# Four buffers for scaled rows and a new order of work in the first chunks of two routed feed-forward stages

## The chip, the cores and the metric

The kernel runs on one core of a Trainium2 chip. The metric is the device time of one execution in microseconds (us), median of the runs. All times in a profile are counted from the start of its span.

## The reference

```python
x = x + 0.5 * ffn(layernorm(x))          # first FFN stage, routed
x = x + attention(layernorm(x))          # 32 sequences of 512 rows, causal, one head of 256
x = x + 0.5 * ffn(layernorm(x))          # second FFN stage, same weights

def ffn(x):                               # T = 16384 rows of 256, E = 8 experts, cap = T // E = 2048
    xn = rmsnorm(x) * norm_weight
    probs = softmax(xn @ router_w.T + router_b)
    gates, idx = top_k(probs.T, cap)      # each expert takes its 2048 best rows
    hmid = gelu(xn[idx] @ fc1_w.T + fc1_b)            # 256 -> 1024, per expert
    ye = hmid @ fc2_w.T + fc2_b                       # 1024 -> 256
    out = zeros.at[idx].add(ye * gates)
    gate_sums = zeros.at[idx].add(gates)
    return out / max(gate_sums, 1e-9)
```

## The kernel before, in words

The program has four parts: a scan of x that gives router logits (to about 85 us), the choice of the rows and the first FFN stage (to about 835 us), attention (to about 1300 us), the choice and the second FFN stage (to the end). The five engines have a program each; they meet through semaphores, and each engine's order of work is written by hand. Products in float32 quality are made of three float16 products (high by high, high by low, low by high), so each value is split into a high and a low half.

**An FFN stage** is 32 chunks of 512 chosen rows, four chunks an expert. In the code N0 and E0 are the first chunk and first expert of the stage, m is the chunk within the stage, and t one of four blocks of a chunk. TensorE runs in block (m, t): two slices of `fc1` of chunk m (12 matmuls, 2.6 us), then `fc2` of chunk m-1 for 128 rows (24 matmuls, 2.6 us). A chunk needs, in this order:

- *its slot list*: TensorE's `pick` (four small matmuls) and VectorE's `count_slots` turn the counts of chosen rows into row numbers (`tok`, `gate_at`). `pick(E, q)` waits for `tiles` and for the `count_slots` of the list before it.
- *its rows*: GpSimd's `gather`, 4 indirect DMAs, into one of two buffers `xe`. It waits for the slot list.
- *its scale* (first stage only, since there the layer norm is still to be made): VectorE's `rows_stats` (4 BN_STATS, 4 BN_AGGR, then `cx`), GpSimd's `roots` (`zsx`, a power of -0.5), VectorE's `rows_shift` (`zbx`).
- *its split rows*: ScalarE's `rows_hi` and VectorE's `rows_lo` write `xs`, and SyncE's queue transposes them into `xt` (`columns`).
- `fc1`, then ScalarE's `gelu` (to `hf` and `hid_h`) and VectorE's `hidden_lo` (`hid_l`), then `fc2`, then VectorE's `y_bias` (`yb`).
- *its gates*: GpSimd's `weights`, 4 indirect DMAs that read the list `gate_d` in DRAM; ScalarE's `y_out` multiplies `yb` by them into the scaled rows `ys`; GpSimd's `scatter`, 4 indirect DMAs, adds `ys` to the rows in DRAM.

ScalarE works in order too. In the first block of chunk m it does two gelus, then the `y_out` that are due there (`scaled(m, t)`: chunk 0's four blocks at (2, 3), chunk 1's at (3, 0) and (3, 1), from chunk 5 on one a block, just behind), then `rows_hi` of chunk m+1, then goes on with gelu. `fc1` slice f writes one of three PSUM banks, so slice 3 of chunk m waits for gelu 0, and slice 5 for gelu 2 of that chunk: two slices can run ahead of a ScalarE that waits.

**The choice for experts 1 to 7** is finished while chunks 0 and 1 already run: `choice_3` to `choice_8` on VectorE, and between them TensorE's `other_limits` at (1, 0) and `other_places` at (1, 3), which waits for `choice_7`. From the finished mask, GpSimd's `gate_sums` and `gates` and VectorE's `gate_scale` make the normalised gates, SyncE writes them to `gate_d`, and `weights` reads them.

GpSimd's order in a stage is the program of `ffn_rows`: one engine issues every gather, weights and scatter DMA and computes the roots, and while it waits for one of them, none behind it starts.

## Time and profile before

| | us |
|---|---|
| median of 3 runs (2070.72 to 2072.58) | 2071.78 |
| the profiled execution | 2071.05 |
| its span | 2069.2 |
| TensorE busy in the span | 1951.3 (94%) |
| VectorE, ScalarE, GpSimd busy | 1449.0, 1398.8, 1259.4 |
| mean granted TensorE clock | 0.98 |

The time of an execution is its span and 1.85 us around it. The profile comes from one execution; 0.98 of the clock is a mean over stretches at full clock and a few at half.

### The profile page before, as it was taken

To read this page: it belongs to the slowest core of one execution; us is meant where nothing else is said; L and a number is where in the kernel's file an instruction comes from. 1 tells how busy PE (TensorE), PEld (TensorE's weight loads), DVE (VectorE), ACT (ScalarE), POOL (GpSimd) and SP (SyncE) were. 2 spreads that over 40 slices of the span, in tenths; PEclk is the share of its full clock that TensorE was granted. 3 is DMA by queue.
4 is the path that set the end of the run, shared out by engine and by line. 5 is a ranking of instruction groups with operands and counts; after the bars stand their busy time and mean duration, and the time that the engine had idled before them with its cause. 6 is when DMAs were issued, how large, how long until landed. Compare 5 with 4: busy or idle time off the path is not lost. (4 is left out here: it accounts for less than half of the span.)

```text
span 2069.2 us, 42505 instructions
## 1 busy us (share of the span) xinstructions
PE 1951.3 (94%) x15382; PEld 1352.3 (65%) x15382; DVE 1449.0 (70%) x4271; ACT 1398.8 (68%) x2680; POOL 1259.4 (61%) x1437
## 2 busy tenths in 40 slices
PE   8858999999999999799999999669999999999997
PEld 6534666666666666577777777435666666666665
DVE  7778777777777765488899998677555555656542
ACT  8635676766767676578888787455576676666663
POOL 8224887777777776644444442027877676767674
PEclk9979999999999999999999999989999999999999
DMA  9943565646565545655555554234655555646453
GB/s 289 346 123 92 114 101 91 106 89 131 85 108 92 100 76 69 116 134 154 159 159 163 135 150 116 85 77 105 107 115 89 107 108 87 131 85 106 71 77 36
DMA packets 361744, 242.33 MB, mean 117 GB/s; under 512 B 228928, under 2 KB 348992, under 8 KB 361280
## 3 DMA queue, kind: packets, MB, share of 16 engines
q1 hardware_dynamic: 304192, 172.34, 31.7%
q0 software_dynamic: 57344, 67.29, 22.4%
q8 instruction: 122, 2.00, 0.4%
q14 instruction: 86, 0.70, 0.1%
HBM read 121.03 MB, written 84.93 MB: 100 GB/s over the span
## 5 line engine op out<-in xcount | busy, mean ns | idle before, releaser
L1273 DVE SCALAR_TENSOR_TENSOR hid_l<-hf,hid_h 128x512 f16<-128x512 f32 x512 | 352.3, 699 | 341.4 <-ACT hid_h L719 340.0
L1494 PE MATMUL ps<-w_h,hid_h 128*128 128x256 f16 x2048 | 559.2, 273 | 0.0
L1495 PE MATMUL ps<-w_l,hid_h 128*128 128x256 f16 x2048 | 559.1, 273 | 0.0
L1496 PE MATMUL ps<-w_h,hid_l 128*128 128x256 f16 x2048 | 558.9, 273 | 0.0
L1494 PE MATMUL ps<-xt,w_h 128*128 128x512 f16 x1024 | 389.8, 381 | 19.4 <-ACT hf L820 14.3
L820 ACT ACTIVATE hf<-ps,b 128x512 f32<-128x512 f32 x512 | 345.1, 674 | 78.5 <-PE ps L1496 72.1
L1496 PE MATMUL ps<-xt,w_l 128*128 128x512 f16 x1024 | 389.9, 381 | 0.0
L1495 PE MATMUL ps<-xt,w_h 128*128 128x512 f16 x1024 | 389.7, 381 | 0.0
L719 ACT ACTIVATE ys<-yb,weight 128x256 f32<-128x256 f32 x256 | 128.0, 506 | 342.6 <-DVE yb L1291 336.2
L719 ACT ACTIVATE hid_h<-hf 128x512 f16<-128x512 f32 x512 | 322.5, 630 | 16.2
L606 POOL DMA_INDIRECT weight<-gate_d,gate_at x256 | 257.7, 1007 | 84.1 <-issue 76.5
L616 POOL DMA_INDIRECT out<-ys,tok x128 | 207.5, 1621 | 113.0 <-ACT ys L719 77.1
L1494 PEld LDWEIGHTS ps<-w_h,hid_h 128*128 128x128 f16 x2048 | 200.8, 98 | 50.5 <-issue 0.5
L1495 PEld LDWEIGHTS ps<-w_l,hid_h 128*128 128x128 f16 x2048 | 200.7, 98 | 50.2 <-issue 0.5
L616 POOL DMA_INDIRECT x_d<-ys,tok x128 | 207.7, 1623 | 37.3 <-issue 36.7
L1496 PEld LDWEIGHTS ps<-w_h,hid_l 128*128 128x128 f16 x2048 | 200.7, 98 | 23.5
L596 POOL DMA_INDIRECT xe<-x,tok x128 | 132.1, 1032 | 103.6 <-DVE gate_at L1228 65.7
L596 POOL DMA_INDIRECT xe<-z_d,tok x128 | 137.2, 1072 | 93.6 <-issue 93.4
L1496 PEld LDWEIGHTS ps<-xt,w_l 128*128 128x128 f16 x1024 | 100.5, 98 | 121.9 <-issue 1.9
L1494 PEld LDWEIGHTS ps<-xt,w_h 128*128 128x128 f16 x1024 | 100.6, 98 | 117.5 <-ACT hf L820 16.8
L1495 PEld LDWEIGHTS ps<-xt,w_h 128*128 128x128 f16 x1024 | 100.5, 98 | 93.6 <-issue 1.4
L1291 DVE TENSOR_TENSOR yb<-ps,b_now 128x256 f32<-128x256 f32 x256 | 107.4, 420 | 62.9 <-PE ps L1496 61.2
(289 smaller groups left out, 3818.1 us busy)
## 6 DMA issues: line engine op xcount, KB each, us to landing
w_st<-fc_t SPq DMA_DIRECT2D x32, 1024.0 KB
xin<-x SPq DMA_DIRECT2D x32, 512.0 KB, 6.1
xa<-x_d SPq DMA_DIRECT2D x32, 512.0 KB, 4.6
out<-x SPq DMA_DIRECT2D x32, 512.0 KB, 5.2
z_d<-z SPq DMA_DIRECT2D x32, 512.0 KB, 6.1
xt<-xs SPq DMA_TRANSPOSE x256
weight<-gate_d,gate_at POOLq DMA_INDIRECT x256, 2.4
b_st<-fc_b SPq DMA_DIRECT2D x16, 128.0 KB
```

Of the source, the lines that this page charges most:

```text
L596: pool.indirect_dma_start(xe[:, n % 2, t, :], None, rows, bass.IndirectOffsetOnAxis(ap=tok[:, E % 3, k:k + 1].bitcast(U32), axis=0)).then_ ...
L606: pool.indirect_dma_start(weight[:, E % 3, k:k + 1], None, gate_d, bass.IndirectOffsetOnAxis(ap=gate_at[:, E % 3, k:k + 1].bitcast(U32), a ...
L616: pool.indirect_dma_start(acc, bass.IndirectOffsetOnAxis(ap=tok[:, E % 3, k:k + 1].bitcast(U32), axis=0), ys[:, n % 2, t, :], None, comput ...
L719: return act.activation(dst, src, ACT.Copy, **kw)
L820: act.activation(hf[:, f % HF, :], bank(FC1[f % 3]), ACT.Gelu, bias=b1[:, e, f:f + 1], scale=1.0 / WS).then_inc(s_gelu, 1)
L1273: dve.scalar_tensor_tensor(hid_l[:, n % 2, f, :], hf[:, f % HF, :], HS, hid_h[:, n % 2, f, :], ALU.mult, ALU.subtract).then_inc(s_hl, 1)
L1291: dve.tensor_tensor(yb[:, n % 2, t, :], bank(4 + t % 2)[:, 0:D], b2_now[:, n // NC % 2], ALU.add).then_inc(s_yb, 1)
L1494: pe.matmul(dst, lh, rh, start=first, stop=False)
L1495: pe.matmul(dst, lh, rl, start=False, stop=False)
L1496: return pe.matmul(dst, ll, rh, start=False, stop=last)
```

## The change

- **Four buffers of scaled rows.** `ys` had two. Two more (`ys_more`) are laid over `above` and `scan`, which are free once the choice is done. Chunk n uses buffer n mod 4, with a semaphore of its own, so `y_out` of chunk n waits for the scatter of chunk n-4, no longer n-2.
- **Gate sum.** GpSimd keeps one multiplication (`chosen`); its three additions go. VectorE adds the eight experts in one reduction over a view of `gate` whose neighbouring elements lie 512 bytes apart. `gate_scale` moves from behind `tiles` at (1, 3) to (1, 2), ahead of `choice_7`.
- **First chunks' slot list, statistics, roots, gathers.** The fourth list (`pick` and `count_slots`) moves from chunk 1 to chunk 0. `rows_stats` of chunk 1 moves ahead of `choice_2` and the low halves of the fc2 weights, that of chunk 3 from the end of (1, 3) to (1, 2). GpSimd gets the order shown below.
- **Scatters.** The chunk in which two are issued is m = 6, was m = 4; the early scatters ahead of the roots go.
- **Weight load swapped.** SyncE issues the second expert's fc2 weights ahead of the store of `gate_d`, not behind it.

```diff
+    YS_RING = 4
...
-            return {2: [0], 3: [1], 4: [2, 3]}.get(m, [m - 1])
+            return {2: [0], 3: [1], 4: [2], 5: [3], 6: [4, 5]}.get(m, [m - 1])
...
+                w2_in(E0 + 1)
                 sp.wait_ge(s_gate, layer + 1)
                 sp.dma_start(gate_d.rearrange("(e t p) a -> t e (p a)", e=NE, p=P), gate[:, :, :]).then_inc(s_gate_d, 16)
-                w2_in(E0 + 1)
...
-            def gate_sums(layer):
+            def chosen(layer):
 
                 pool.wait_ge(s_mask, layer + 1)
-                steps.link(pool.tensor_tensor(gate[:, :, :], equal[:, :, :], p_r[:, :, :], ALU.mult))
-                steps.link(pool.tensor_tensor(gsum[:, :, :], gate[:, 0:NE // 2, :], gate[:, NE // 2:NE, :], ALU.add))
...
+                pool.tensor_tensor(gate[:, :, :], equal[:, :, :], p_r[:, :, :], ALU.mult).then_inc(s_gsum, 1)
...
+                roots(N0 + 1)
                 gather(N0 + 2)
-                roots(N0 + 1)
                 roots(N0 + 2)
-                gate_sums(layer)
                 gather(N0 + 3)
+                chosen(layer)
+                roots(N0 + 3)
                 gates(layer)
-                roots(N0 + 3)
+                gather(N0 + 4)
                 pool.wait_ge(s_gate_d, 16 * (layer + 1))
                 weights(N0)
                 weights(N0 + 1)
...
                 for m in range(2, LAST + 1):
-                    if m + 2 < LAST:
+                    if 4 <= m and m + 2 < LAST:
                         gather(N0 + m + 2)
                     if m < LAST:
                         weights(N0 + m)
-                    early = scattered(m)[:1] if m in (3, 4) else []
-                    for n in early:
-                        scatter(N0 + n)
                     if m + 2 < LAST:
                         roots(N0 + m + 2)
+                    if m == 2:
+                        gather(N0 + 5)
...
-                        for n in scattered(m)[len(early):]:
+                        for n in scattered(m):
                             scatter(N0 + n)
...
-                link(dve.tensor_scalar(ginv[:, :], gsum[:, 0, :], 1e-9, None, ALU.max))
+                link(dve.tensor_reduce(ginv[:, :], gate[:, :, :].rearrange("p e t -> p t e"), AX.X, ALU.add))
+                link(dve.tensor_scalar(ginv[:, :], ginv[:, :], 1e-9, None, ALU.max))
...
+                    if (m, t) == (0, 3):
+                        count_slots(0, E0, 3)
...
                     if (m, t) == (1, 1):
                         choice_6(layer)
-                        count_slots(0, E0, 3)
                     if (m, t) == (1, 2):
+                        rows_stats(E0 * NC + 3)
+                        gate_scale(layer)
                         choice_7(layer)
                     if (m, t) == (1, 3):
                         choice_8(layer)
                         tiles(1, E0 + 1, 0, 1)
-                        gate_scale(layer)
...
                 count_slots(0, E0, 2)
+                rows_stats(N0 + 1)
```

GpSimd in the first stage, from the roots of chunk 3 to those of chunk 4. `xe<-x,tok` is a gather, `weight<-gate_d,gate_at` a weights DMA, `zsx<-cx` a roots. Before:

```order
L582 TENSOR_TENSOR gate<-gate,ginv 128x1024 [waits s_ginv]
L623 TENSOR_TENSOR zsx<-cx,minus_half 128x4 [waits s_cx]
L606 DMA weight<-gate_d,gate_at 128x1 [waits s_gate_d,s_idx]
L606 DMA weight<-gate_d,gate_at 128x1 x3
L606 DMA weight<-gate_d,gate_at 128x1 [waits s_idx]
L606 DMA weight<-gate_d,gate_at 128x1 x3
L596 DMA xe<-x,tok 128x256 [waits s_xsl,s_copy,s_idx]
L596 DMA xe<-x,tok 128x256 x3
L606 DMA weight<-gate_d,gate_at 128x1 [waits s_idx]
L606 DMA weight<-gate_d,gate_at 128x1 x3
L623 TENSOR_TENSOR zsx<-cx,minus_half 128x4 [waits s_cx]
```

And after:

```order
L624 TENSOR_TENSOR zsx<-cx,minus_half 128x4 [waits s_cx]
L583 TENSOR_TENSOR gate<-gate,ginv 128x1024 [waits s_ginv]
L597 DMA xe<-x,tok 128x256 [waits s_idx,s_xsl]
L597 DMA xe<-x,tok 128x256 x3
L607 DMA weight<-gate_d,gate_at 128x1 [waits s_gate_d,s_idx]
L607 DMA weight<-gate_d,gate_at 128x1 x3
L607 DMA weight<-gate_d,gate_at 128x1 [waits s_idx]
L607 DMA weight<-gate_d,gate_at 128x1 x3
L607 DMA weight<-gate_d,gate_at 128x1 [waits s_copy,s_idx]
L607 DMA weight<-gate_d,gate_at 128x1 x3
L624 TENSOR_TENSOR zsx<-cx,minus_half 128x4 [waits s_cx]
```

Chunk 4's gather stood behind the weights of chunks 0 and 1 and now stands ahead of them. It waits (`s_idx`) for the first slot list of expert 1, made in block (2, 1), and all three weights and the roots of chunk 4 stand behind it.

VectorE in the first stage, block (1, 2), up to the row that releases `other_places` (the third after the scan). `hid_l` is `hidden_lo`, `seen` to `gate_at` a `count_slots`, `bstx` to `cx` a `rows_stats`. Before, from the end of (1, 1):

```order
L1215 TENSOR_SCALAR seen,found<-ps,slot_id 128x127 [waits s_pick,s_mask]
L1215 TENSOR_SCALAR seen,found<-ps,slot_id 128x127 x3
L1219 TENSOR_TENSOR tok_f<-found,ps 128x4 [waits s_dve]
L1227 CAST tok<-tok_f 128x4 [waits s_seen]
L1228 TENSOR_SCALAR gate_at<-tok_f,first_row 128x4
L1273 SCALAR_TENSOR_TENSOR hid_l<-hf,hid_h 128x512 [waits s_hh] x2
L1291 TENSOR_TENSOR yb<-ps,b_now 128x256 [waits s_y]
L1180 SCALAR_TENSOR_TENSOR scan<-equal 128x896
```

And after:

```order
L1275 SCALAR_TENSOR_TENSOR hid_l<-hf,hid_h 128x512 [waits s_hh,s_mask]
L1275 SCALAR_TENSOR_TENSOR hid_l<-hf,hid_h 128x512 [waits s_hh]
L1293 TENSOR_TENSOR yb<-ps,b_now 128x256 [waits s_y]
L1250 BN_STATS bstx<-xe 128x6 [waits s_xe1]
L1250 BN_STATS bstx<-xe 128x6 x3
L1253 BN_AGGR mvx<-bstx 128x2 [waits s_dve]
L1253 BN_AGGR mvx<-bstx 128x2 x3
L1255 TENSOR_SCALAR cx<-mvx 128x4 [waits s_dve]
L1196 TENSOR_REDUCE ginv<-gate 128x128 [waits s_gsum]
L1197 TENSOR_SCALAR ginv<-ginv 128x128 [waits s_dve]
L1198 RECIPROCAL ginv<-ginv 128x128 [waits s_dve]
L1199 TENSOR_SCALAR ginv<-ginv 128x128 [waits s_dve]
```

The slot list has left this place for chunk 0; chunk 3's statistics and the whole gate scale now stand ahead of the scan. In the second stage the same holds without `bstx` to `cx`.

GpSimd in the first stage, chunk 6, with the first rows of chunk 7. Before, one scatter stands between the roots of chunk 8 and the gather of chunk 9; after, there are two:

```order
L624 TENSOR_TENSOR zsx<-cx,minus_half 128x4 [waits s_cx]
L617 DMA x_d<-ys,tok 16384x256 [waits s_ys]
L617 DMA x_d<-ys,tok 16384x256 x3
L617 DMA x_d<-ys,tok 16384x256 [waits s_ys]
L617 DMA x_d<-ys,tok 16384x256 x3
L597 DMA xe<-x,tok 128x256 [waits s_idx,s_xsl]
L597 DMA xe<-x,tok 128x256 x3
```

Those rows are of the changed program; the four scatter DMAs of chunk 5 are what moved in ahead of the gather.

## Rows read from the trace of the kernel before

**Rows 1.** Busy time by stretch: length, PE, PEld, DVE, ACT, POOL, clock, DMA share, GB/s

```profile
200.00:250.00 50.00, 45.45 (x307) 29.92 (x305) 39.46 (x125) 30.36 (x54) 38.01 (x34) 0.93 0.54 121
350.00:400.00 50.00, 50.00 (x356) 34.35 (x355) 35.98 (x111) 36.53 (x63) 35.14 (x31) 1.00 0.46 85
1400.00:1450.00 50.00, 45.35 (x312) 30.10 (x310) 38.97 (x98) 29.90 (x55) 37.56 (x30) 0.97 0.46 106
```

**Rows 2.** TensorE's timeline, first stage: start, duration, operation, idle before and releaser

```profile
191.60 0.39 PE L1620 MATMUL ps<-per_expert,before 128*128 128x7 f32 x2 [1.44 <-DVE per_expert L1182]
208.07 0.61 PE L1494 MATMUL ps<-xt,w_h 128*128 128x512 f16 x1 [4.13 <-ACT hf L820]
...
231.81 0.38 PE L1494 MATMUL ps<-xt,w_h 128*128 128x512 f16 x1
...
246.96 0.40 PE L1659 MATMUL ps<-counts,tile_of 128*128 128x128 f16 x4 [0.42 <-DVE tile_of L1208]
...
255.46 0.39 PE L1494 MATMUL ps<-xt,w_h 128*128 128x512 f16 x1 [1.60 <-ACT hf L820]
261.97 0.38 PE L1659 MATMUL ps<-counts,tile_of 128*128 128x128 f16 x4 [2.42 <-DVE tok_f L1219]
```

**Rows 3.** TensorE's timeline, second stage

```profile
1424.72 0.55 PE L1494 MATMUL ps<-xt,w_h 128*128 128x512 f16 x1 [4.62 <-ACT hf L820]
...
1491.20 0.39 PE L1494 MATMUL ps<-xt,w_h 128*128 128x512 f16 x1 [0.77 <-ACT hf L820]
```

**Rows 4.** ScalarE's timeline, both stages

```profile
206.81 0.63 ACT L719 ACTIVATE w_h<-w_st 128x512 f16<-128x512 f32 x1 [2.54 <-DMA w_st<-fc_t]
...
1415.22 1.33 ACT L719 ACTIVATE xs<-xe 128x256 f16<-128x256 f32 x4 [3.09 <-DMA xe<-z_d,tok]
1423.46 0.63 ACT L719 ACTIVATE w_h<-w_st 128x512 f16<-128x512 f32 x1 [6.90 <-DMA w_st<-fc_t]
...
1488.85 0.51 ACT L719 ACTIVATE ys<-yb,weight 128x256 f32<-128x256 f32 x1 [6.38 <-DMA out<-ys,tok]
```

**Rows 5.** VectorE's timeline, first stage; its last row is of the second

```profile
167.11 1.08 DVE L1163 TENSOR_REDUCE per_expert<-above 128x7 f32<-128x896 f32 x1
...
188.86 2.21 DVE L1180 TENSOR_TENSOR_SCAN scan<-equal 128x896 f32<-128x896 f32 x1
...
195.76 0.95 DVE L1196 RECIPROCAL ginv<-ginv 128x128 f32<-128x128 f32 x1
...
212.51 0.39 DVE L1228 TENSOR_SCALAR gate_at<-tok_f,first_row 128x4 int32<-128x4 f32 x1
...
1429.12 0.22 DVE L1228 TENSOR_SCALAR gate_at<-tok_f,first_row 128x4 int32<-128x4 f32 x1
```

**Rows 6.** GpSimd by line, 188 to 400 us; then one row of its timeline

```profile
L616 POOL DMA_INDIRECT x_d<-ys,tok x37 | 61.2, 1654 | 10.4 <-issue 10.1 <-ACT ys L719 0.3
L606 POOL DMA_INDIRECT weight<-gate_d,gate_at x44 | 44.5, 1011 | 15.2 <-issue 13.1 <-DMA gate_d<-gate 2.1
...
250.84 1.62 POOL L623 TENSOR_TENSOR zsx<-cx,minus_half 128x4 f32<-128x4 f32 x1
```

**Rows 7.** GpSimd's roots of chunk 8; gathers' and weights' landing; VectorE, chunk 7's end

```profile
313.08 1.05 POOL L623 TENSOR_TENSOR zsx<-cx,minus_half 128x4 f32<-128x4 f32 x1 [2.77 <-DVE cx L1253]
...
DMA to landing us min/median/max: 2.7/3.0/3.3
...
weight<-gate_d,gate_at POOLq DMA_INDIRECT x256, 2.4
...
331.38 1.39 DVE L1248 BATCH_NORM_STATS2 bstx<-xe 128x6 f32<-128x256 f32 x4
...
334.55 0.43 DVE L1208 TENSOR_TENSOR tile_of<-tile_of,below 128x512 f16<-128x512 f16 x1
```

**Rows 8.** Busy time by stretch, as rows 1, around two idle times of TensorE

```profile
209.00:220.00 11.00, 11.00 (x70) 7.35 (x69) 7.79 (x21) 8.11 (x16) 8.30 (x9) 0.81 0.50 155
1424.00:1429.00 5.00, 4.28 (x18) 2.31 (x19) 2.95 (x12) 4.87 (x10) 3.78 (x5) 0.66 0.36 59
```

More of the change, by code:

```diff
@@ L183, in macaron @@
         gate = sb("gate", [P, NE, P], F32, ffn)
-        gsum = sb("gsum", [P, NE // 2, P], F32, ffn)
         ginv = sb("ginv", [P, P], F32, ffn)
@@ L190, in macaron @@
         p_r = sb("p_r", [P, NE, P], F32, ffn)
-        above = sb("above", [P, NE, P], F32, ffn)
         equal = sb("equal", [P, NE, P], F32, ffn)
-        scan = sb("scan", [P, NE, P], F32, ffn)
+        choice = ExitStack()
+        above = sb("above", [P, NE, P], F32, choice)
+        scan = sb("scan", [P, NE, P], F32, choice)
+        choice.close()
+        ys_more = sb("ys_more", [P, 2, TG, D], F32, ffn)
         w1_h = sb("w1_h", [P, 2, KD, FF], F16, ffn)
@@ L299, in macaron @@
         s_xe = [sem("s_xe0"), sem("s_xe1")]
-        s_sc = [sem("s_sc0"), sem("s_sc1")]
+        s_sc = [sem(f"s_sc{u}") for u in range(YS_RING)]
         s_xt = [sem("s_xt0"), sem("s_xt1")]
@@ L361, in final_rows @@
             for n in (FINAL - NC + g - 1, FINAL - NC + g):
-                engine.wait_ge(s_sc[n % 2], 16 * TG * (n // 2 + 1))
+                engine.wait_ge(s_sc[n % YS_RING], 16 * TG * (n // YS_RING + 1))
         def flat(t):
@@ L707, in _ @@
             ffn_rows(1, z_d, outf)
-            for u in range(2):
-                pool.wait_ge(s_sc[u], 16 * TG * NC * NE)
+            for u in range(YS_RING):
+                pool.wait_ge(s_sc[u], 16 * TG * (2 * NC * NE // YS_RING))
             pool.sem_inc(s_phase, 1)
@@ L842, in y_out @@
                         act.wait_ge(s_weight[c], 16 * TG * (E + 1))
-                        wait(act, s_sc[n % 2], 16 * TG * (n // 2))
+                        wait(act, s_sc[n % YS_RING], 16 * TG * (n // YS_RING))
                     act.wait_ge(s_yb, TG * n + t + 1)
-                    copy(ys[:, n % 2, t, :], yb[:, n % 2, t, :], scale=weight[:, E % 3, k:k + 1]).then_inc(s_ys, 1)
+                    copy(scaled_rows(n)[:, t, :], yb[:, n % 2, t, :], scale=weight[:, E % 3, k:k + 1]).then_inc(s_ys, 1)
                 act.activation(warm[:, :], nws[:, 0:1], ACT.Gelu)
@@ L1221, in count_slots @@
                 if q == 0:
-                    for u in range(2):
-                        wait(dve, s_sc[u], 16 * TG * (NC // 2) * (E - 2))
+                    for u in range(YS_RING):
+                        wait(dve, s_sc[u], 16 * TG * (NC // YS_RING) * (E - 2))
                     for c in range(NC):
@@ L1348, in ffn @@
                     w2_lo(E0, h)
-                rows_stats(N0 + 1)
                 for m in range(LAST + 1):
@@ L1366, in ffn @@
                             first_turns(m, t)
-                        if t == 3 and m + 2 < LAST:
+                        if t == 3 and m + 2 < LAST and m != 1:
                             rows_stats(n + 2)
@@ L1682, in ffn @@
                             pick(ahead, 2 * c + t // 2)
+                        if (m, t) == (0, 1):
+                            pick(E0, 3)
                         if (m, t) == (1, 0):
                             other_limits(layer)
-                            pick(E0, 3)
                         if (m, t) == (1, 3):
```

9 lines of the change are left out of this document (3 added, 6 removed).

## The prediction

> **What bounds the kernel now.** I read the busy time by stretch first. In steady state, 350 to 400 us, TensorE (PE) is busy for all of 50.00 us at a granted clock of 1.00, the upper of its two levels (2.4 GHz), and no other engine passes 36.53 [rows 1]. There only TensorE's own work counts, and the change leaves that alone. What can move are the two heads: 200 to 250 us has 4.55 us of idle TensorE and a clock of 0.93, 1400 to 1450 us 4.65 us and 0.97 [rows 1]. Then TensorE's timeline, for the names of these idle times. First stage: 1.44 us until VectorE's per-expert counts of choice_7, 4.13 until a gelu at 208.07, and in chunk 4 0.42, 1.60 and 2.42 [rows 2]. Second stage: 4.62 at 1424.72 and 0.77 at 1491.20, both until a gelu [rows 3]. ScalarE's timeline says why the gelus are late: it had waited for the fc2 weights of the second expert, 2.54 us at 206.81 and 6.90 at 1423.46, for the gather of chunk 3 (3.09 at 1415.22), and for a scatter to free one of the two buffers (6.38 at 1488.85) [rows 4]. After the two long idle times the clock falls to the lower level (1.2 GHz) for a while: 11.00 us at a mean of 0.81 and 5.00 at 0.66 [rows 8], which cost (1 - 0.81) x 11 = 2.1 us and (1 - 0.66) x 5 = 1.7 us.
>
> So the question is for which of the other engines TensorE waits in the two heads after the change. A chunk takes TensorE four blocks of 5.2 us and a few picks, about 21 us. A move is worth something only where it shortens or lengthens one of its waits.
>
> **Block (1, 2), first stage.** Moved ahead of choice_7 on VectorE: rows_stats of chunk 3, 2.0 us (1.39 for its BN_STATS, as at 331.38 [rows 7], 0.6 for the aggregates), and the gate scale: reciprocal 0.95 [rows 5] and two short operations, 1.4 in all, and the new reduction over 1024 elements. The trace has no reduction with elements 512 bytes apart; the nearest row reduces 896 elements in 1.08 us [rows 5], so 1024 take 1.23. Above it the bound is the slowest VectorE rate over such a tile, the scan, 2.21 for 896 [rows 5], so 2.5; below, 1.1. I take 1.23, since the work is of the kind of the first row. Sum 4.6. Gone from ahead of choice_7 is the slot list, 2.55 us here (1.7, and 0.85 for one slow CAST), of which VectorE would now spend up to 1.1 waiting for gelus, so it gives back 1.45 to 2.55: choice_7 ends 2.1 to 3.2 later. I take 2.4, 193.9 and not 191.5, and TensorE, which idled 1.44 [rows 2], idles 2.4 more. An idle time of 3.8 us is close to the 4.13 that had the lower level behind it [rows 8], so I add 1.7 for clock: **+4.1**. The other three waits of this head go: gather 3 stands no more behind the gate sums, and the weights are loaded ahead of the store, so the 4.13 and the 2.1 of clock vanish, **-6.2**.
>
> **Chunk 3, first stage.** The largest term. GpSimd now issues gather 4 ahead of weights 0, 1, 2 and of the roots of chunk 4. Gather 4 needs the first slot list of the second expert, which ended in before at 212.51 + 0.39 = 212.9 [rows 5]. It ends VectorE's chain, from which 3.4 us (rows_stats, gate scale) are gone behind choice_7, which itself is 2.4 later; with what the clock gives or takes I leave it at 212.4. Weights 0 to 2, which before did not wait for that list, now do. First issue 0.85 later, as elsewhere behind a list, 213.3. Sixteen DMAs: 1.01 us busy each [rows 6] and 0.3 between them, 1.31 x 16 = 21.0; the roots start at 234.3 and end at 235.3 (1.05, as [rows 7]). From there ScalarE's rows_hi and two gelus have to come: in before roots ended at 250.84 + 1.62 = 252.46 [rows 6] and TensorE went on at 255.46 [rows 2], 3.0 later. So slice 5 of chunk 3 starts at 238.3, where it was 231.81 [rows 2]. TensorE, 2.1 us ahead of before until there, then stands still for some 8.6 us. Against before that is +6.5, and the clock behind it costs about what it did behind the 4.13, 2.0; 0.2 are taken off for a pick that comes later. Chunk 4 starts **+8.3**. This is counted from the program's start and so contains the two terms of the paragraph above (-2.1); it doesn't add to them.
>
> Queued behind the roots is all that TensorE needs: ScalarE works in order, its rows_hi of chunk 4 waits for them, and its gelus stand behind rows_hi, so only two fc1 slices run ahead.
>
> **Chunk 4.** Its idle times of 0.42, 1.60 and 2.42 [rows 2] came from roots behind an early scatter of 4 x 1.95 us [rows 6] and from VectorE. The scatter goes; of 4.44 us I leave 1.2 for VectorE's tile row: **-3.2**.
>
> **Chunk 6.** Two scatters now stand between the roots of chunk 8 and gather 9. Write C for the statistics of chunk 8 (the roots' start, 313.08 in before [rows 7]). Roots and the gap take 1.25, eight scatter DMAs 8 x 1.95 = 15.6, four gathers 5.2 less the last gap, and the last row lands 3.0 after its issue [rows 7], in all C + 23.8. VectorE wants these rows at 331.38 [rows 7], which is C + 18.3. It stands in order behind that wait, 5.4 us late, and with it the tile rows (334.55 [rows 7]) that TensorE's next pick needs; the pick has 1.1 us of slack: 4.3 of stall, 0.8 at the next pick, and some clock: **+5.8**. In the second stage no statistics exist and nothing waits so early: 0.
>
> **Second stage.** The waits on weights, gather and buffer go: 4.62 + 0.77 [rows 3] + 1.7 of clock = 7.1. Against it: chunk 2's y_out now waits for weights 0 behind the slot list, which stands at 1429.34 in before [rows 5] and 6.9 earlier with the stalls gone, 1422.4; 0.85 to the issue, eight issues and a landing of 2.4 [rows 7] make 1435.3 for weights 0, which leaves gelus 1.1 to 1.4 late; and 0.7 for other_places and a pick. **-5.4**.
>
> **At nothing.** The statistics of chunk 1 move ahead of work that VectorE does before rows_shift of chunk 1 in either order. The fourth slot list (1.7 us) in chunk 0 delays the roots of chunk 2 by as much; without cover it would cost those 1.7, but slice 5 of chunk 1 comes some 5 us behind them. Four buffers: the same DMAs and products at other addresses. The moved load puts 1 MB ahead of the store of gates; the store's readers, weights 0, stand behind the slot list at 213.3, some 15 us after the gates, so the cover is wide (without it, the first weights waited 2.1 us in before [rows 6]).
>
> **Sum.** +8.3 - 3.2 + 5.8 - 5.4 = +5.5 us. On the profiled 2071.05 that is 2076.6; the median is 0.7 above the profiled one: **2077.3 us**.
>
> **Rivals.**
> *Chunk 3's roots don't reach TensorE* (faster). If the slot list comes by about 204, or sixteen issues need 0.8 us each and not 1.31, the roots end by 228 and the stall is gone. Then -2.1 stands in place of +8.3: -2.1 - 3.2 + 5.8 - 5.4 = -4.9, 2066.9 us. For it: the list depends on VectorE, which I move by less than 1 us on thin grounds. Against: 1.31 is a mean of 44 rows. 0.15.
>
> *The double scatter hides in VectorE's slack*: +5.8 falls away, -0.3, 2071.5 us. For it: gather 9 may be issued between if scaled rows of chunk 5 come late or early enough; VectorE in steady state is busy for 35.98 of 50 us [rows 1] and can catch up. Against: its wait is in order. 0.2.
>
> *The reduction is slow*: 2.5 and not 1.23, ahead of choice_7 in both stages, where TensorE already waits: 2 x 1.3 = +2.6, 2079.9 us. For: elements 512 bytes apart. Against: no row here slows with such a view. 0.1.
> The Trainium skill, page "SBUF — State Buffer", section on Door 1, says SBUF has lines of 16 bytes and "each access that crosses to a new line pays a penalty"; the view crosses at each element. It gives no price; no run here shows it yet.
>
> *The second stage keeps its wait*: had the fc2 weights landed late for another reason than the store ahead of them (they share the transfer engines with gathers), the -5.4 is gone: +10.9, 2082.7 us. For: 6.90 us of wait [rows 4] were blamed on the load alone. Against: the order of the queue. 0.05.
>
> **How the numbers follow.** The forecast as it stands has 0.5. Its own range, from both ends of the costs: list 2 us earlier or later (2.0), clock terms 0 or double (1.7 to 2.1 each), chunk 6 between 3 and 7: 2072 to 2082. The range for 8 in 10 reaches to the first rival below and the last above: 2067 to 2083. A measurement here tells apart about 0.2%, 4.1 us: 2067.7 to 2075.9 is "same". Slower: most of the forecast (0.4), the slow reduction and the kept wait, in round terms 0.50. Faster: the first rival (0.15) and a tail of the second, 0.18. Same: the rest, 0.32.
>
> **What the changed profile would show.** Right: TensorE idle near 190 us for 3 to 5 us until per_expert; no idle time at 208; one of 7 to 10 us at slice 5 of chunk 3, near 238, until a gelu, with ScalarE waiting on zsx and GpSimd issuing without a gap before it; in chunk 7 one of 4 us at a pick with tile_of as releaser and BN_STATS waiting for xe; in the second stage no wait above 2 us on w_st. Wrong: the roots of chunk 4 end before 228; the gather of chunk 9 lands before its statistics are due; the reduction's row is above 2 us; or gaps between GpSimd's issues are other than 0.3.

## The result, and the profile after

The changed kernel takes 2086.27 us (median of four runs, 2084.59 to 2089.18) beside 2072.18 of the kernel before on the same chip: ratio 1.0070, 95% interval 1.0054 to 1.0086. It is slower by 14 us. That is the forecast's side, and 3 us outside its range of 2067 to 2083. The profiled execution has a span of 2082.8 us, 13.6 more. Medians here and below are those of the fast runs; left out are one run of `repaired` (2583.27 us at a mean granted clock of 0.75) and one of the kernel before (5613.31 us).

TensorE's idle times of 0.15 us and over from 155 us on in the first stage and from 1405 us on in the second, from its timeline (start, duration, operation, idle before and releaser):

```profile
159.60 0.61 PE L1498 MATMUL ps<-xt,w_h 128*128 128x512 f16 x1 [3.14 <-ACT hf L821]
166.76 0.39 PE L1498 MATMUL ps<-xt,w_h 128*128 128x512 f16 x1 [1.73 <-DMA xt<-xs]
195.71 0.60 PE L1624 MATMUL ps<-per_expert,before 128*128 128x7 f32 x2 [7.57 <-DVE per_expert L1183]
214.29 0.38 PE L1663 MATMUL ps<-counts,tile_of 128*128 128x128 f16 x4 [0.24 <-DVE tok_f L1221]
229.51 0.39 PE L1498 MATMUL ps<-xt,w_h 128*128 128x512 f16 x1 [2.90 <-ACT hf L821]
239.50 0.39 PE L1498 MATMUL ps<-xt,w_h 128*128 128x512 f16 x1 [2.94 <-ACT hf L821]
244.40 0.38 PE L1663 MATMUL ps<-counts,tile_of 128*128 128x128 f16 x4 [0.81 <-DVE tok_f L1221]
255.69 0.40 PE L1663 MATMUL ps<-counts,tile_of 128*128 128x128 f16 x4 [0.49 <-DVE tile_of L1210]
344.81 0.61 PE L1663 MATMUL ps<-counts,tile_of 128*128 128x128 f16 x4 [4.59 <-DVE tile_of L1210]
358.89 0.38 PE L1663 MATMUL ps<-counts,tile_of 128*128 128x128 f16 x4 [0.64 <-DVE tok_f L1221]
...
1425.41 0.60 PE L1624 MATMUL ps<-per_expert,before 128*128 128x7 f32 x2 [3.79 <-DVE per_expert L1183]
1456.04 0.39 PE L1498 MATMUL ps<-xt,w_h 128*128 128x512 f16 x1 [0.58 <-ACT hf L821]
1571.85 0.38 PE L1663 MATMUL ps<-counts,tile_of 128*128 128x128 f16 x4 [0.74 <-DVE tok_f L1221]
```

The idle times of 4.13 [rows 2] and of 4.62 and 0.77 us [rows 3] are gone. In their place stand 7.57 (it was 1.44) and 3.79 at choice_7, a pair of 2.9 in chunk 3, and 4.59 at the first pick of chunk 8. Idle time is not the whole price, since the granted clock falls behind the long ones. Busy time by stretch (length, PE, PEld, DVE, ACT, POOL, clock, DMA share, GB/s) around three of them:

```profile
196.00:201.00 5.00, 5.00 (x18) 2.13 (x18) 4.19 (x11) 1.50 (x3) 0.00 (x0) 0.60 0.35 105
344.00:351.00 7.00, 6.19 (x23) 2.90 (x24) 3.08 (x9) 1.79 (x4) 6.16 (x5) 0.56 0.86 207
1425.00:1430.00 5.00, 4.59 (x16) 2.07 (x17) 4.20 (x12) 1.30 (x2) 0.13 (x1) 0.66 0.37 105
```

The lower clock cost (1 - 0.60) x 5 = 2.0 us in the first, at most (1 - 0.56) x 7 = 3.1 in the second, which starts inside the idle time, and (1 - 0.66) x 5 = 1.7 in the third.

So I read each kernel by the time at which TensorE starts a chunk, counted from its start of chunk 0 of the stage. This table is worked out from TensorE's timelines (every 48th of the fc1 matmuls starts a chunk) and shows the difference to the kernel before in us; it takes the clock in, and leaves out what differs ahead of the stage.

```
first stage, start of chunk    2     3     4     5     7     8     9
changed kernel              +6.3  +1.9 +10.7  +6.5  +6.1  +6.1 +14.2
forecast                    +4.1  -2.1  +8.3  +5.1  +5.1  +5.1 +10.9
scale_behind                -0.5  +0.4 +10.1  +5.9  +5.4  +5.4 +13.6
gates_wait                  +5.1  +1.0 +11.4  +7.2  +6.7  +6.7 +14.9
weights_first               +6.4  +1.5  +1.6  -2.7  -3.2  -3.2  +4.7
scatter_spread              +6.4  +1.6 +11.3  +7.0  +6.5  +6.5  +8.5
repaired                    -1.0  -0.4  +1.4  -2.7  -3.2  -3.2  -0.7

second stage                   2     3     4     5     6     7     8     9
changed kernel              +3.8  -1.2  -0.3  -0.3  -1.6  -1.6  -1.6  -0.7
scale_behind                -0.5  -2.6  -1.7  -1.7  -3.0  -3.0  -3.0  -0.7
gates_wait                  +1.7  -3.2  -2.2  -2.2  -3.6  -3.6  -3.6  -2.0
weights_first               +3.6  -1.2  -1.2  -1.2  -2.5  -2.5  -2.5  -2.5
scatter_spread              +3.6  -2.9  -2.0  -2.0  -3.4  -3.4  -3.4  -3.4
before_swap                 -0.0  -5.9  -5.9  -5.9  -0.1  -0.1  -0.1  -0.1
before_swap_sum             -0.3  -5.0  -5.0  -5.0  -0.0  -0.0  -0.0  -0.0
before_ring4                +0.1  +1.0  +1.0  +1.0  -0.4  -0.4  -0.4  -0.4
before_swap_ring4           +0.1  -5.8  -5.8  -5.8  -7.2  -2.8  -2.8  -2.8
repaired                    -0.5  -5.2  -5.2  -5.2  -6.5  -6.5  -6.5  -6.5
```

In the changed kernel nothing more is lost from chunk 9 of the first stage to its end. In the second stage 0.9 us are lost between chunks 8 and 9 and 0.2 behind them, so it ends 0.5 us early. The 0.9 belong to chunk 6's two scatters, which the forecast put at nothing in this stage: they stand ahead of the weights that ScalarE wants there,

```profile
1564.49 0.51 ACT L720 ACTIVATE ys_more<-yb,weight 128x256 f32<-128x256 f32 x1 [5.26 <-DMA weight<-gate_d,gate_at]
```

and the loss is absent in `scatter_spread` and in `weights_first`. Ahead of the first stage the changed kernel's execution is 2.0 us shorter and between the stages, nearly all of it attention, where the change does nothing, 1.9 longer. The profiles of the other kernels differ from that of the kernel before there too (0.3 to 2.5 us shorter ahead, from 1.0 shorter to 2.7 longer between), which is why the table counts from each stage's chunk 0.

### The profile page after: what moved, and what is told of

It reads as the page before. It is cut to its first block, busy times and chain, and to the rows that moved or that the text cites. A ratio compares the mean times of both kernels' runs of the same rounds, so it can differ in the third digit from the quotient of the medians.

```text
span 2082.8 us, 42514 instructions
## 1 busy us (share of the span) xinstructions
PE 1955.8 (94%) x15382; PEld 1352.0 (65%) x15382; DVE 1453.9 (70%) x4273; ACT 1398.7 (67%) x2680; POOL 1249.3 (60%) x1431
## 4 chain that ended last, share of the span: by engine, by line
PE 71%; DVE 8%; issue 7%; POOL 6%; ACT 5%; DMA 1%; SPq 1%; DVEq 0%; POOLq 0%; ACTq 0%
PE ps L1498 22%; PE ps L1500 22%; PE ps L1499 22%; ACT zt_l L720 2%; POOL xe L597 2%; POOL weight L607 2%; POOL x_d L617 1%; PE ps L1716 1%; ACT zt_h L720 1%; DVE hid_l L1275 1%; PE ps L1590 1%; DVE bst L1006 1%; POOL out L617 1%; DMA weight<-gate_d,gate_at 1%; PE ps L1745 1%
## 5 line engine op out<-in xcount | busy, mean ns | idle before, releaser
L720 ACT ACTIVATE ys_more<-yb,weight 128x256 f32<-128x256 f32 x128 | 64.2, 506 | 193.0 <-DVE yb L1293 177.5
L720 ACT ACTIVATE ys<-yb,weight 128x256 f32<-128x256 f32 x128 | 63.9, 506 | 172.2 <-DVE yb L1293 152.2
L617 POOL DMA_INDIRECT out<-ys,tok x64 | 103.4, 1615 | 56.3 <-ACT ys L720 40.8
```

Source lines behind the costliest of these rows:

```text
L617: pool.indirect_dma_start(acc, bass.IndirectOffsetOnAxis(ap=tok[:, E % 3, k:k + 1].bitcast(U32), axis=0), scaled_rows(n)[:, t, :], None, c ...
L720: return act.activation(dst, src, ACT.Copy, **kw)
```

## The experiments

Each is compared with the kernel before on its own chip (2071.9 to 2072.4 us); 95% intervals are those of the ratio.

**The gate scale behind choice_7** (`scale_behind`)

```diff
-                        rows_stats(E0 * NC + 3)
-                        gate_scale(layer)
                         choice_7(layer)
+                        rows_stats(E0 * NC + 3)
+                        gate_scale(layer)
```

> The changed kernel with two lines moved: in block (1, 2) the statistics of chunk 3 and the whole gate scale stand behind choice_7, no longer ahead of it. Theory A (each stall has its own chain; the one in block (1, 2) is order on VectorE): the row that releases other_places comes some 5.3 us earlier (1.94 + 3.27), TensorE's idle times of 7.57 (first stage) and 3.79 us (second) go to under 1. In the second stage nothing stands behind it, so 3.8 and about 1.7 of clock come back. In the first stage chunk 3 then waits for the roots of chunk 4, which follow the slot list of the second expert; that list has the same VectorE work ahead of it as now, so chunk 4 starts at most 2 us earlier. Sum -5.5 to -7.5: about 2080 us. Theory B (the idle times simply add up): 7.57 + 2 of clock + 3.79 + 1.7 = -15, about 2071 us.

2083.25 us, ratio 1.0052 (1.0038 to 1.0066): 3 us less than the changed kernel, with an interval that overlaps its own. The 7.57 and 3.79 us become 0.35 and nothing. But of the 6.8 us gained at chunk 2 only 0.6 are left at chunk 4, because the roots of chunk 4 come only 1.8 us earlier (233.66, was 235.47): the first stage went as theory A has it. In the second stage theory A is wrong: 1.4 us came back by chunk 8, not 5.5, and by chunk 9 nothing. The scale now holds up the low halves that fc2 needs, as TensorE's timeline shows, with the lower clock behind it (mean 0.66 over 5 us):

```profile
1425.49 0.33 PE L1498 MATMUL ps<-w_h,hid_h 128*128 128x256 f16 x1 [2.46 <-DVE hid_l L1275]
```

**GpSimd's gates wait until choice_7 is done** (`gates_wait`)

```diff
                 pool.wait_ge(s_ginv, layer + 1)
+                pool.wait_ge(s_aux, 4 * layer + 4)
```

> The changed kernel with one wait more: GpSimd's multiplication by the gate scale (gates) starts only when choice_7 has ended; VectorE's order stays. Theory A (a part of choice_7's lateness is that the two engines get in each other's way: the copy of 128x6 took 2.12 us and not 0.24 while gates ran 3.99 and not 2.34): copy 0.24 again, choice_7 1.9 us earlier in both stages, TensorE's idle times 7.57 and 3.79 become 5.7 and 1.9; 2082 to 2083 us. Theory B (the long copy has nothing to do with GpSimd, only VectorE's order counts): copy still about 2 us, 2086 us.

2082.29 us, 1.0050 (1.0036 to 1.0063), again with an interval that overlaps the changed kernel's, so the reading goes by the profiles. VectorE's timeline of the changed kernel, from the low halves in (1, 2) to the copy in choice_7:

```profile
182.37 3.45 DVE L1275 SCALAR_TENSOR_TENSOR hid_l<-hf,hid_h 128x512 f16<-128x512 f32 x2
185.74 0.41 DVE L1293 TENSOR_TENSOR yb<-ps,b_now 128x256 f32<-128x256 f32 x1
186.07 1.39 DVE L1250 BATCH_NORM_STATS2 bstx<-xe 128x6 f32<-128x256 f32 x4
187.50 0.38 DVE L1253 BATCH_NORM_AGGREGATE mvx<-bstx 128x2 f32<-128x6 f32 x4
187.91 0.17 DVE L1255 TENSOR_SCALAR cx<-mvx 128x4 f32<-128x4 f32 x1
187.99 1.86 DVE L1196 TENSOR_REDUCE ginv<-gate 128x128 f32<-128x1024 f32 x1
189.89 0.23 DVE L1197 TENSOR_SCALAR ginv<-ginv 128x128 f32<-128x128 f32 x1
190.15 0.95 DVE L1198 RECIPROCAL ginv<-ginv 128x128 f32<-128x128 f32 x1
191.14 0.23 DVE L1199 TENSOR_SCALAR ginv<-ginv 128x128 f32<-128x128 f32 x1
191.28 2.02 DVE L1181 TENSOR_TENSOR_SCAN scan<-equal 128x896 f32<-128x896 f32 x1
193.33 2.12 DVE L1182 COPY per_expert<-scan 128x6 f32<-128x6 f32 x1
```

and GpSimd's over the same time:

```profile
182.42 2.85 POOL L579 TENSOR_TENSOR gate<-equal,p_r 128x1024 f32<-128x1024 f32 x1 [4.46 <-DVE equal L1177]
188.16 1.04 POOL L624 TENSOR_TENSOR zsx<-cx,minus_half 128x4 f32<-128x4 f32 x1 [2.89 <-DVE cx L1255]
191.44 3.99 POOL L583 TENSOR_TENSOR gate<-gate,ginv 128x1024 f32<-128x1024 f32 x1 [2.24 <-DVE ginv L1199]
```

The two low halves take 3.45 us beside the first multiplication (1.29 for two at 178.58, with nothing beside them), and a copy of six elements takes 2.12 and ends at 195.45, just as the second multiplication does (195.43). With `gates` held back the copy and the multiplication are

```profile
194.31 0.17 DVE L1183 COPY per_expert<-scan 128x6 f32<-128x6 f32 x1
```

```profile
194.83 2.65 POOL L584 TENSOR_TENSOR gate<-gate,ginv 128x1024 f32<-128x1024 f32 x1 [4.65 <-DVE per_expert L1184]
```

Theory A holds: the long copy was GpSimd's doing. The two low halves behind it now overlap the multiplication and take 3.43 us, where they took 1.29 in the changed kernel. TensorE's idle times are 6.47 and 1.84, which is 1.1 and 1.95 less. In the first stage that is lost again by chunk 4; in the second 1.95 hold to chunk 8, and 1.3 to the stage's end. The page "GPSIMD Engine Reference" of the Trainium skill says in its section "Key points" that GpSimd shares its SBUF interfaces with VectorE, with contention where VectorE's instruction has two SBUF inputs or runs in a 2-port mode. The low halves have two such inputs, and the trace agrees for them; the copy has one, and no run here shows in which mode it ran. The scan has two as well and keeps its 2.02 us; there it is GpSimd's multiplication that takes longer, 3.99 us where it took 2.34 in the kernel before, with next to no work of VectorE's beside it. The scan had started first (191.28 and 191.44), and the copy, started while the multiplication ran, ends with it: this looks like one engine waiting for the other, not like both going slower, but no run was made to tell the two apart.

**Weights 0 and 1 ahead of the gather of chunk 4** (`weights_first`)

```diff
                 gates(layer)
-                gather(N0 + 4)
                 pool.wait_ge(s_gate_d, 16 * (layer + 1))
                 weights(N0)
                 weights(N0 + 1)
+                gather(N0 + 4)
```

> The changed kernel with the gather of chunk 4 behind weights 0 and 1, where the kernel before has it, all else as changed. Theory A (chunk 3 waits since roots of chunk 4 stand behind sixteen DMAs that all wait for one slot list): roots of chunk 4 end near 226 and not at 236.5, the two idle times of 2.90 and 2.94 us and 0.8 behind them go, chunk 4 starts 6 to 7 us earlier, second stage 0.6: about 2079.5 us. Theory B (TensorE would wait there anyway, for VectorE's late rows and lists behind choice_7): under 2 us, 2085 us.

2074.87 us, 1.0015 (1.0006 to 1.0024), 11 us less than the changed kernel. In the changed kernel the two idle times of chunk 3 have two different causes, as ScalarE's timeline shows: the first gelu of the chunk stands behind chunk 0's `y_out`, which waits for weights 0, and the third behind `rows_hi` of chunk 4, which waits for the roots.

```profile
226.66 1.70 ACT L720 ACTIVATE ys<-yb,weight 128x256 f32<-128x256 f32 x4 [8.02 <-DMA weight<-gate_d,gate_at]
...
236.81 2.07 ACT L812 ACTIVATE xs<-xe,zbx,zsx 128x256 f16<-128x256 f32 x4 [4.20 <-DVE zbx L1261]
```

The roots of chunk 4 on GpSimd, in this run

```profile
225.50 1.05 POOL L624 TENSOR_TENSOR zsx<-cx,minus_half 128x4 f32<-128x4 f32 x1
```

and in the changed kernel

```profile
215.32 1.24 POOL L597 DMA_INDIRECT xe<-x,tok  x1 [19.89 <-DVE gate_at L1230]
...
235.47 1.05 POOL L624 TENSOR_TENSOR zsx<-cx,minus_half 128x4 f32<-128x4 f32 x1
```

GpSimd had sat idle for 19.89 us until the slot list, with eight DMAs behind that gather that needed nothing of that list. Both idle times of chunk 3 go, since both the weights and the roots come earlier; chunk 4 starts 9.1 us earlier (6 to 7 were expected), and the second stage ends 1.9 us earlier (0.6 expected). Theory A, and the largest single part of the loss.

**The second scatter spread over chunks 6 to 9** (`scatter_spread`)

```diff
-            return {2: [0], 3: [1], 4: [2], 5: [3], 6: [4, 5]}.get(m, [m - 1])
+            return {2: [(0, 0, 4)], 3: [(1, 0, 4)], 4: [(2, 0, 4)], 5: [(3, 0, 4)], 6: [(4, 0, 4), (5, 0, 1)],
+                    7: [(5, 1, 4), (6, 0, 2)], 8: [(6, 2, 4), (7, 0, 3)], 9: [(7, 3, 4), (8, 0, 4)]}.get(m, [(m - 1, 0, 4)])
```

> The changed kernel with the second scatter of chunk 6 spread: five scatter DMAs in each of chunks 6, 7 and 8 and nine... one more per chunk until chunk 9 has caught up (4 + 1, 3 + 2, 2 + 3, 1 + 4), instead of eight in chunk 6. Theory A (eight scatters between the roots of chunk 8 and gather 9 make its statistics, and with them the tile row, late): gather 9 is issued 5.8 us earlier, the idle time of 4.59 us at the pick of chunk 8 and the half clock behind it go, 8 us: about 2078 us. Theory B (the pick waits for VectorE's own backlog, the gather only shares it): idle time stays above 2 us, 2083 us or more.

2081.21 us, 1.0043 (1.0030 to 1.0057), 5 us less. The profiled execution is the fastest of the five, 2076.14. The changed kernel's VectorE waits for the rows of chunk 9,

```profile
341.12 1.41 DVE L1250 BATCH_NORM_STATS2 bstx<-xe 128x6 f32<-128x256 f32 x4 [5.65 <-DMA xe<-x,tok]
```

and in this run the same instruction starts at 335.81 without a wait. The idle time of 4.59 is gone, one of 1.83 at a later pick is left; between chunks 8 and 9 the kernel loses 2.0 us and not 8.1, and in the second stage nothing where it lost 0.9. Theory A, with a rest. The 1.7 us that its second stage is ahead at chunk 3 are clock: behind the same idle time of 3.79 us at choice_7 the granted clock stayed at 1.00 in this execution.

**Single edits on the kernel before** (`before_swap`, `before_swap_sum`, `before_ring4`, `before_swap_ring4`). The first has only the swap:

```diff
+                w2_in(E0 + 1)
                 sp.wait_ge(s_gate, layer + 1)
...
-                w2_in(E0 + 1)
```

> The kernel before with the one edit that the fc2 weights of the second expert are loaded ahead of the store of gates. Theory A (the load is what ScalarE waits for, 2.54 and 6.90 us): neither wait is there; first stage: the 4.13 us shrink to under 2, but the idle times of chunk 4 are set by GpSimd's order and take most of that back (0 to -2 at chunk 5); second stage: the 4.62 us and 1.7 of clock go, -6: 2064 to 2066 us. Theory B (the load is slow for another reason, the gathers beside it): waits over 2 us stay, 2071 us.

2072.37 us, 1.0000 (0.9992 to 1.0009). The waits for the weights are gone, and chunk 3 of the second stage starts 5.9 us earlier. At chunk 6 nothing of it is left: theory A was right on the waits and wrong on the time. ScalarE's timeline there:

```profile
1487.73 0.51 ACT L719 ACTIVATE ys<-yb,weight 128x256 f32<-128x256 f32 x1 [10.21 <-DMA out<-ys,tok]
```

In the kernel before this wait for a buffer was 6.38 us [rows 4]. Without the stall ahead of it, it grew by 3.8, and TensorE's idle time there from 0.77 to 4.75. In the first stage nothing is gained even at chunk 3: where 4.13 us stood there are 1.56 and, at the pick at 212.04, 3.09; in chunk 4 stand 2.87 and the lower clock where 1.60 stood, and chunk 5 starts 1.6 us late.

The second adds VectorE's reduction, `gate_scale` at its old place, GpSimd without its three additions:

```diff
+                link(dve.tensor_reduce(ginv[:, :], gate[:, :, :].rearrange("p e t -> p t e"), AX.X, ALU.add))
+                link(dve.tensor_scalar(ginv[:, :], ginv[:, :], 1e-9, None, ALU.max))
```

> As before_swap, and the gate sum by one VectorE reduction in the old place of the gate scale, at the end of (1, 3); GpSimd keeps the one multiplication, so the gather of chunk 3 comes 4.9 us earlier. Theory A (the reduction costs VectorE 1.9 us off the path and frees GpSimd): same as before_swap or up to 2 us better, 2062 to 2066 us. Theory B (VectorE's 1.9 us delay the rows of chunk 3, which TensorE waits for): 1 to 3 us worse than before_swap.

2073.53 us, 1.0006 (0.9997 to 1.0015): not to be told from `before_swap`. In the second stage the gather of chunk 3 comes earlier (first DMA at 1402.70, was 1408.43 in `before_swap`) and ScalarE's wait for its rows goes from 2.95 to 0.32 us, but the first slot list of the second expert is late instead (1.58 us at that pick, where `before_swap` has 0.41). Neither theory is borne out beyond the noise. This profile also shows the multiplication `chosen` (182.63, 2.35 us) beside a slot list and not beside low halves: only the list's CAST grows, and it ends with the multiplication, at 185.0, while the low halves behind take 1.28 us.

```profile
183.98 1.02 DVE L1222 CAST tok<-tok_f 128x4 int32<-128x4 f32 x1
...
185.05 1.28 DVE L1268 SCALAR_TENSOR_TENSOR hid_l<-hf,hid_h 128x512 f16<-128x512 f32 x2
```

The third has only the four buffers (`YS_RING = 4`, `ys_more`, and the semaphores):

> The kernel before with four buffers of scaled rows and nothing else of the change. Theory A (y_out waited 6.38 us for a scatter in the second stage, and TensorE 0.77 and 0.23 behind it): these waits go, -1.0 to -1.3 in the second stage, 0 in the first: about 2070.8 us. Theory B (the wait is hidden or comes back at the next list): no difference, 2072 us.

2072.28 us, 1.0001 (0.9992 to 1.0009). In the profile chunk 6 of the second stage gains 1.3 us on chunk 5, as theory A has it, but chunk 3 had lost 1.0; the median shows no gain. The fourth has buffers and swap:

> The kernel before with two edits of the change, the weight load swapped and four buffers; GpSimd's and VectorE's orders stay. Alone neither moved the median (2072.4 and 2072.3 beside 2072.4). Theory A (in the second stage the swap gains 5.9 us at chunk 3 and TensorE loses them at chunk 5, where y_out waits for one of two buffers; four take that wait away): no idle time at chunk 5, chunk 6 starts 6 to 7 us ahead of the kernel before, first stage unchanged within 1.5: 2065 to 2067 us. Theory B (the 4.75 us at chunk 5 are due to the weights or the slot list behind them, not to the buffers): idle time there stays, 2072 us.

2069.81 us, 0.9986 (0.9978 to 0.9995): a gain, of 2.3 us and not the 5 to 7 of theory A. The idle time of chunk 5 is gone, and chunk 6 starts 7.2 us early, more than the 5.9 - 5.8 + 1.3 of the parts: the swap alone only uncovers the wait that the buffers take away. One chunk later 4.4 us are lost. This kernel still has GpSimd's old order, with two scatters in chunk 4, and they put the weights that ScalarE wants behind eight scatter DMAs and a gather. On GpSimd and on ScalarE:

```profile
1483.83 1.62 POOL L624 DMA_INDIRECT out<-ys_more,tok  x1 [0.30 <-issue]
...
1508.31 0.95 POOL L614 DMA_INDIRECT weight<-gate_d,gate_at  x1 [0.30 <-issue]
```

```profile
1510.56 0.51 ACT L727 ACTIVATE ys<-yb,weight 128x256 f32<-128x256 f32 x1 [6.82 <-DMA weight<-gate_d,gate_at]
```

The profiled execution is the slowest of the twelve, 2074.20 us; it also loses 4.0 us in chunk 12 of the first stage, where ScalarE waits 4.38 us for weights and TensorE 2.17 at a pick (431.91). What delays those weights was not looked into.

**The three orders mended together** (`repaired`): the edits of `weights_first` and `scatter_spread`, and on VectorE

```diff
                     if (m, t) == (1, 2):
-                        rows_stats(E0 * NC + 3)
-                        gate_scale(layer)
                         choice_7(layer)
+                        rows_stats(E0 * NC + 3)
...
                         tiles(1, E0 + 1, 0, 1)
+                        gate_scale(layer)
```

> The changed kernel with the gather of chunk 4 behind weights 0 and 1, the second scatter spread over chunks 6 to 9, and VectorE's order in the first chunks so: choice_7, then the statistics of chunk 3 in (1, 2); choice_8, tiles, then the gate scale in (1, 3). Theory A (three separate orders cost the time, and what is left of the change gains): no idle time above 1 us ahead of other_places in either stage, none in chunk 3, under 1 us at the pick of chunk 8; chunk 9 starts 1 to 5 us ahead of the kernel before, the second stage is 4 to 6 us shorter than before: 2062 to 2068 us. Theory B (gate work has to collide with something: moved to (1, 3) it holds the low halves of chunk 1's last slices and the rows of chunk 3 up, and TensorE waits at chunk 2 as in the run with the scale behind choice_7, 5.62 and 2.46 us): 2069 to 2073 us.

2065.45 us, 0.9967 (0.9955 to 0.9980): 21 us less than the changed kernel and 7 less than the kernel before, in the range of theory A. The second stage keeps all 6.5 us; the first is within 1, less than theory A had. The longest idle times left in the first stage from chunk 2 on, on TensorE's timeline:

```profile
205.21 0.39 PE L1499 MATMUL ps<-xt,w_h 128*128 128x512 f16 x1 [3.45 <-ACT hf L822]
...
212.36 0.38 PE L1664 MATMUL ps<-counts,tile_of 128*128 128x128 f16 x4 [1.39 <-DVE tok_f L1222]
...
344.29 0.38 PE L1664 MATMUL ps<-counts,tile_of 128*128 128x128 f16 x4 [2.25 <-DVE tok_f L1222]
```

**Two attempts at the rest** (`later_catch_up`, `shift_early`), both on top of `repaired`. The first puts the scatters that lag in chunks 8 and 9:

```diff
+            return {**{m: [(m - 2, 0, 4)] for m in range(2, 8)}, 8: [(6, 0, 4), (7, 0, 2)],
+                    9: [(7, 2, 4), (8, 0, 4)]}.get(m, [(m - 1, 0, 4)])
```

> The kernel called repaired, with the scatters caught up in chunks 8 and 9 (six DMAs each), no longer spread over 6 to 9. The gathers behind them are those of chunks 11 and 12, whose statistics come in chunks 9 and 10, and chunks 10 and 11 need no slot list. Theory A (a late gather costs only where a slot list stands behind its statistics): the 2.25 us at chunk 8 and some 1.2 of clock go, nothing comes in their place, 2062 to 2064 us. Theory B (VectorE late by 3.9 us holds the low halves up as well, wherever it is): an idle time of 2 to 4 us at chunk 10 or 11 in its place, 2065 us or more.

2067.15 us, 0.9978 (0.9969 to 0.9988), no better than `repaired`. The 2.25 us at chunk 8 went (chunk 9 starts 3.4 us ahead of the kernel before, in `repaired` 0.7), and came back in chunks 11 and 12: ScalarE waits 5.00 us for weights, TensorE 2.48 at a pick at 430.48, and the stage ends 2.1 us behind the kernel before, in `repaired` 0.7 ahead. Theory A is wrong in that nothing comes in its place. GpSimd's timeline from one gather to the next, with 0.3 us between issues throughout and no wait:

```profile
405.44 1.02 POOL L598 DMA_INDIRECT xe<-x,tok  x1 [0.30 <-issue]
...
424.99 1.10 POOL L598 DMA_INDIRECT xe<-x,tok  x1 [0.30 <-issue]
```

A chunk of GpSimd's work takes 19.55 us of TensorE's 20.9. By an estimate from these two it regains 1.3 us a chunk, so four scatters (7.8 us) are a backlog of about six chunks. How much of the loss in chunk 12 that backlog makes is open: `before_swap_ring4`, which catches up in chunk 4, lost 4.0 us in the same place in its profile.

The second attempt moves two pieces of VectorE's work:

```diff
+                        if (m, t) == (1, 3):
+                            rows_shift(n + 2)
...
+                            if m == 2 and t >= 2:
+                                w1_lo(ahead, t - 2)
```

> later_catch_up, and VectorE's rows_shift of chunk 3 goes ahead of choice_8 in (1, 3), and the low halves of the second expert's first weights from (2, 0) and (2, 1) to (2, 2) and (2, 3). Theory A (what is left in chunk 2 are a gelu behind rows_hi of chunk 3, 3.45 us, and a pick behind VectorE's backlog, 1.39): the first goes, the second grows by what VectorE doesn't get rid of (1.3 of its work moves behind the list): the two together fall from 4.8 to 3 us or less, with less of half clock behind: 2 to 3 us less than later_catch_up in the first stage, 1 in the second. Theory B (the first slot list of the second expert comes at 212 whatever is done, and TensorE waits for it): under 1 us.

2068.09 us, 0.9979 (0.9970 to 0.9988): no gain. The 3.44 us at a gelu of chunk 2 went and the pick behind it waits 4.00 and not 1.57: theory B for the first stage; in the second, chunk 9 starts 0.6 us earlier than in `later_catch_up`. VectorE has no idle time of its own from 186 us to 215, behind the list, so it looks as if only less work on it would help there.

**The price of the view** (`sum_twice`): a second reduction ahead of the real one, over neighbours; its result is overwritten.

```diff
+                link(dve.tensor_reduce(ginv[:, :], gate[:, :, :].rearrange("p e (t k) -> p (e t) k", k=NE), AX.X, ALU.add))
                 link(dve.tensor_reduce(ginv[:, :], gate[:, :, :].rearrange("p e t -> p t e"), AX.X, ALU.add))
```

> The changed kernel with one reduction more, ahead of that of the gate sum: same tile, same 1024 inputs and 128 outputs, but over eight neighbours, so no 512-byte steps (its result is overwritten). It prices the view alone. Theory A (the steps of 512 bytes cost: 1.86 to 1.93 us and not the 1.23 that the row over 896 neighbours gives): this one takes 1.2 to 1.3 us. Theory B (short groups of eight cost, not the steps): also 1.9 us. The time as a whole rises by its length in each stage, 2 to 4 us.

2089.56 us in one run, which says nothing on the time; the rows are what it was made for. VectorE's timeline:

```profile
188.08 1.21 DVE L1196 TENSOR_REDUCE ginv<-gate 128x128 f32<-128x1024 f32 x1
189.33 1.87 DVE L1197 TENSOR_REDUCE ginv<-gate 128x128 f32<-128x1024 f32 x1
```

Theory A: the same number of inputs and outputs, and 0.66 us for the steps of 512 bytes. In the second stage it is 1.20 and 1.94.

## Why the prediction was wrong

The sign was right and so was most of the mechanism; the sum was +5.5 and the profiles give +13.6, which is 8.1 more. By the table the step that failed most is the second stage, +4.9 over its forecast; next are block (1, 2) with the waits that go, +4.0, and chunk 6's scatters, +2.3. Chunks 3 to 7 together came out 3.0 below. By the prediction's own steps:

- **Second stage (-5.4): the step that failed.** It came out at -0.5. The 7.1 us of waits did go, but "0.7 for other_places and a pick" stands where the same gate scale ahead of choice_7 costs 3.79 of idle time and 1.7 of clock. The first stage's working was not carried over, because there the statistics of chunk 3 had been half of the sum. The scale and GpSimd's hold-up alone are enough. `gates_wait` gives 1.3 of it back by the stage's end, `repaired`, with the scale in its old place, all of it. The nothing for chunk 6's scatters in this stage was 0.9.
- **Block (1, 2) (+4.1, of it 2.4 idle): right in place, low by 3.7 in idle time.** TensorE idles 7.57, 6.1 more than before. The working summed VectorE's durations as if nothing ran beside them. Three terms of it failed: the low halves (3.45, in before 2.36 beside the gate sums, so +1.1), the reduction (1.86 and not 1.23, +0.6), and the copy (2.12 and not 0.24, +1.9); 3.6 together. The middle one is the rival of the slow reduction, half way between its two bounds. The other two are GpSimd's multiplications, which the trace of before could have told of: its two low halves at 186.24 and its CAST of 1.01 us stand beside the gate sums. The prediction called that CAST slow and didn't ask why.
- **The waits that go (-6.2): right.** At chunk 3 the kernel is 4.4 us better off than at chunk 2, with 2.0 of clock behind the new idle time inside it.
- **Chunk 3 (+8.3): the order on GpSimd was right, the picture of the stall was not.** Chunk 4 starts 10.7 us late, of which 1.9 were there at chunk 3: the chunk itself loses 8.8 us, and the forecast had 8.3 + 2.1 = 10.4. The sixteen DMAs, their 1.25 to 1.31 us each and the gelu behind rows_hi are as described, and `weights_first` takes 9.1 us back. But one idle time of 8.6 us at slice 5 was expected, and there are two of 2.9, each with a cause of its own. The first is at slice 3, behind the `y_out` that waits for weights 0; the prediction weighs that wait in the second stage and leaves it out here. The list came at 214.5 and not 212.4, in a program that was 2.0 us ahead. Why is only half known: in `scale_behind` TensorE has choice_7's counts 7.2 us earlier, and GpSimd the list only 2.0. That the roots still ended near the forecast (236.5 and 235.3) is in part luck.
- **Chunk 4 (-3.2): right**, 4.2.
- **Chunk 6's two scatters (+5.8): right in the mechanism, low by 2.3.** The rows land 23.6 us behind the start of the roots of chunk 8 (23.8 said), and the pick waits 4.59 (4.3 said); the lower clock behind it was priced at under 1 us, and the window above says up to 3.1.
- **Four buffers and the swap: nothing as a cost was right.** Weights 0 don't wait for the store of `gate_d` in the changed kernel; in `weights_first`, where they come sooner, they wait 4.04 us. The statistics of chunk 1 and the fourth slot list, also put at nothing, cost little: chunk 1 starts 0.2 us late, and nothing stands between there and choice_7. What the two bring was priced in -6.2 and -5.4, and the runs show that it takes both: the swap brings 5.9 us at chunk 3 and loses them without the buffers, and in `repaired` 6.5 stay.
- **Rivals.** Roots that don't reach TensorE are refuted by the idle time at 239.50, whose gelu stands behind them (that at 229.51 is the weights'), a double scatter that hides by that at 344.81. A second stage that keeps its wait: the waits for weights and buffer went, and another took their place, at its price.

What stays open: how much of `gates_wait`'s first-stage gain would show if nothing stood behind it, which was not tried, and what `chosen` beside other work than the low halves would bring the changed kernel; in `before_swap_sum` it cost VectorE some 0.85 us where beside the low halves it costs 2.2. Open too is why the clock stayed up behind one idle time of 3.79 us and fell behind the same one in two other kernels.

## What to carry to other kernels

Ahead of a move on an engine that issues in order, look at what the instruction waits for, and count all behind it that doesn't need that: here eight DMAs that didn't need a slot list stood behind a gather whose list was 20 us away. Price a moved piece again in each place that it runs in, since the second stage runs the same code without the work that hid or outweighed it. Two edits that each bring nothing can bring something together (here 2.3 us in the median, 7.2 at chunk 6 of the second stage), when one uncovers the wait that the other takes away; time them as a pair before dropping either.
